# A LoRA layer and a top-2 mixture of experts in one launch: the residual folded into the first layer's weights, x1's two parts taken straight from PSUM, x first on SyncE's queue

## The chip, the cores and the metric

The kernel runs on one core of a Trainium2 chip. The metric is the device time of one launch in microseconds (us). TensorE (PE) multiplies matrices into PSUM, VectorE (DVE) and ScalarE (ACT) work on PSUM and SBUF, GpSimd (POOL) on SBUF only, and SyncE (SP) issues most transfers. Each engine runs its own instructions in order, and the engines meet at semaphores, which the program waits on and raises by hand: nothing reorders the work.

## The reference

Sixteen sequences x of 128 rows by 128 features go through two residual layers, all in float32.

```python
# layer 0, for each sequence b:  W_base, 8 pairs (As[e], Bs[e]) of rank 16, weights cond_8[b, e]
x1 = x + x @ W_base.T + b_base + 2 * sum_e cond_8[b, e] * (x @ As[e].T) @ Bs[e].T
# layer 1: softmax over cond_8[b], the two largest kept and normalised -> w[b, e]
mlp(x1; g, u, d) = (gelu(x1 @ g) * (x1 @ u)) @ d          # 128 -> 512 -> 128
out = x1 + mlp(x1; shared) + sum over the two experts e of b: w[b, e] * mlp(x1[b]; e)
```

## The kernel before

Before anything is computed, layer 0 is rewritten as one weight per sequence: `delta_w(g)` (L906 to L911, on PE) multiplies `a_sb` by `sB`, which is B transposed and scaled by the sequence's weights, for a group g of four sequences (GB = 4, NG = 4 groups), one bank of PSUM each. `w_eff(g)` (DVE) adds the transposed base weight `wT` and leaves the sum in `work`. PE also transposes x itself (`x_transposes`, L904) and ACT copies the result into `xT` (`copy_xT`). Then PE's `first_layer(g)` (L918) multiplies the two into bank 4 + g, and DVE's `first_layer(g)` (L673) adds the bias and the residual `xT` and writes x1 over `xn`. This opening stage ends when x1 is split into a high part (`x1_hi`, float32 rounded to the matmul format) and a low part (`x1_lo`, the remainder). ACT and DVE do that for group 0, ACT and POOL for group 1, and POOL alone for groups 2 and 3, in `x1_split`.

The second stage is the shared MLP. `shared_group(g)` runs over four chunks c of 128 hidden columns, so a step t = 4g + c has three matmuls for the gate and three for the up projection (L985 to L987: high by high, high by low, low by high), and three for the down projection of the chunk two steps earlier (L1001 to L1003). ACT applies gelu, DVE multiplies (`gated`), ACT and DVE split the product (`split_h_hi`, `split_h_lo`). Between these stand parts of a small sort, by POOL and a few tiny matmuls, which deals the 32 pairs of sequence and expert into 12 slots of two sequences that share an expert, and 8 singles. `sort_counts` is the first of them, and DVE packs the lists into words (`pack`), which each engine loads into registers (`read`, L243). In the same stage ACT, DVE and POOL split the experts' weights into `wex`.

The third stage is four singles (`gate_up_single` L1043, `down_single` L1061), then twelve slots (`slot`, L1079 to L1081 and L1101 to L1103), then four more singles and the output. PE's addresses for the first four down projections come from `downs_of(0)`, a read of the word `four_e`. It stands in `shared_group` behind the gate and up matmuls of the last step and ahead of `down_shared(3, 1)`; `downs_of(1)` stands between `gate_up_single(3)` and `down_single(2, ...)`.

SyncE's queue begins with B (`b_nat`, 1,024 runs of 64 bytes), then group 0 of x, W_base, x group 1, the shared gate weights and so on; ACT's queue brings cond_8, As and the bias. ACT loads the table for exp before the router's softmax, and the table for gelu (L541) just before the shared stage.

Of the kernel before, what the change touches and what calls it, by code (L numbers as in the profile page):

```python
# [17 lines left out]
def lora_then_top2_moe(nc, x, cond, W_base, b_base, As, Bs, ex_gate, ex_up, ex_down,  # L18
# [31 lines left out]
    with ExitStack() as ctx:  # L50
# [66 lines left out]
        with nc.sbuf_tensor("sB", [P, 2, GB, H], F32) as sB:  # L117
            pass
# [47 lines left out]
        sB_ready = sem("sB_ready")  # L166
        xT_ps = sem("xT_ps")
# [6 lines left out]
        x1lo_first = sem("x1lo_first")  # L174
        x1lo_later = sem("x1lo_later")
# [78 lines left out]
        def _(sp):  # L254
            sp.dma_start(b_nat[:, :, :], Bs.rearrange("e o r -> o e r")).then_inc(ld_b, 16)
# [75 lines left out]
        def _(pool):  # L331
# [33 lines left out]

            pool.wait_ge(sh_hi, 1)
# [21 lines left out]
            x1_split(1)  # L388
            pool.wait_ge(x1_ready, NG)
# [34 lines left out]
            x1_split(2)  # L424
            up_lo(0, 1)
            x1_split(3)
# [23 lines left out]
            for k in range(2):  # L450
                for i, value in enumerate((top_idxf[:, k:k + 1], bcol[:, 0:1], rt[:, 22 + k:23 + k])):
                    pool.tensor_scalar(rows[:, k, i, :], iota[:, :], lp[:, 12 + k:13 + k], value,
                                       ALU.is_equal, ALU.mult).then_inc(sort_step, 1)
            up_lo(2, 4)
            up_lo(3, 5)
            up_lo(4, 5)
# [24 lines left out]
            pool.wait_ge(x1lo_first, 1)  # L481
            pool.wait_ge(x1lo_later, NG - 1)
# [26 lines left out]
        def _(act):  # L509
            act.dma_start(cond_sb[:, :], cond).then_inc(ld_cond, 16)  # L510
            act.dma_start(a_sb[:, :], As.rearrange("e r c -> (e r) c")).then_inc(ld_a, 16)
# [16 lines left out]
            copy_xT(0)  # L528
            copy_xT(1)
# [3 lines left out]
            copy_xT(2)  # L533
            split_x1_hi(0)

            act.wait_ge(ld_sh_up, 16)
            act.copy(wsh[:, 2 * I:3 * I], raw_sh[:, 1, :]).then_inc(sh_hi, 1)
            copy_xT(3)
            split_x1_hi(1)

            act.activation(rt[:, 24:25], rt[:, 8:9], ACT.Gelu_apprx_tanh).then_inc(gelu_table, 1)  # L541
# [50 lines left out]
            def slot(p, j):  # L592
                for n in range(2):
# [4 lines left out]
                    if n == 0:  # L598
# [11 lines left out]
            act.wait_ge(lists_ready, 2)  # L610
            for p in range(NBUF):
# [9 lines left out]
        def _(dve):  # L621
# [12 lines left out]
            def router_weights():  # L634
# [4 lines left out]
                dve.tensor_scalar(rt[:, 16:18], rt[:, 8:10], rt[:, 2:3], None, ALU.mult).then_inc(rt_step, 1)  # L639
                dve.wait_ge(rt_step, 6)  # L640
# [11 lines left out]
            def scale_B(g, bT=bT):  # L652

                if g >= 2:
                    dve.wait_ge(delta_ps, g - 1)
                dve.tensor_tensor(sB[:, g % 2, :, :],
# [12 lines left out]
            def first_layer(g):  # L669

                dve.wait_ge(x1_ps, g + 1)
                dve.wait_ge(xT_ready, g + 1)
                dve.scalar_tensor_tensor(xn[:, g * GB:(g + 1) * GB, :],  # L673
                                         bank[4 + g][:, :].rearrange("p (b s) -> p b s", b=GB), bias[:, 0:1],
                                         xT[:, g * GB:(g + 1) * GB, :], ALU.add, ALU.add).then_inc(x1_ready, 1)
# [8 lines left out]
            scale_B(1)  # L684
# [505 lines left out]
```

## Time and profile before

| what | value |
|---|---|
| median of 3 runs | 133.23 us (133.16 to 133.29) |
| the profiled execution's own time | 133.25 us |
| its span, first to last instruction | 131.6 us |
| PE busy | 125.8 us, 96% of the span |
| DVE, ACT, POOL busy | 89.9, 70.5, 59.4 us |
| share of PE in the chain that ended last | 86% |
| bytes moved | 26.56 MB, mean 202 GB/s |

The profiled execution's own time is 1.65 us above its span, and 0.02 us above the median, so that a difference worked out in the span can be taken off the median as it is. PE is busy nearly everywhere. What can be won lies in the opening stage, in which PE waits for others and its matmuls are longer, and in the few gaps behind it.

### The profile page before, as it was taken

How to read it: one execution, taken by the hardware profiler on the slowest of the kernel's cores; microseconds unless marked ns; L12 is line 12 of the kernel's file. 1: busy time of each engine (PE TensorE's matmuls, PEld its weight loads, DVE VectorE, ACT ScalarE, POOL GpSimd, SP SyncE). 2: the span in 40 equal slices, each digit the busy share in tenths (PEclk: the TensorE clock that was granted, in tenths of full speed). 3: DMA queues.
4: the chain of work that ended last, by engine and by line, in shares of the span. 5: the costliest groups of instructions: out<-in, count | busy, mean ns of one | idle time of the engine just before them, and what ended most of it. 6: DMA issues, size and time to landing. Idle time of an engine off the chain costs nothing.

```text
span 131.6 us, 3151 instructions
## 1 busy us (share of the span) xinstructions
PE 125.8 (96%) x869; PEld 113.9 (87%) x869; DVE 89.9 (68%) x180; ACT 70.5 (54%) x134; POOL 59.4 (45%) x110
## 2 busy tenths in 40 slices
PE   6999999999999997999989999999999999999991
PEld 6657787878887867999989999999999999999991
DVE  2678879679977888643375677666867686766741
ACT  3431867977856874411284665666566755711110
POOL 5209285497785737352065325633463504610000
PEclk9999999999999999999999999999999999999999
DMA  3997888799100077469835875577599970013921
GB/s 55 278 332 271 229 264 237 237 293 298 47 2 0 0 216 252 143 248 404 344 120 199 319 279 204 202 281 299 199 308 328 396 224 0 2 29 136 272 70 56
DMA packets 14524, 26.56 MB, mean 202 GB/s; under 512 B 2224, under 2 KB 7600, under 8 KB 12976
## 3 DMA queue, kind: packets, MB, share of 16 engines
q1 hardware_dynamic: 14192, 26.35, 60.1%
q8 instruction: 5, 0.08, 0.3%
q10 hardware_dynamic: 320, 0.07, 0.2%
q14 instruction: 7, 0.06, 0.1%
HBM read 12.52 MB, written 1.31 MB: 105 GB/s over the span
## 4 chain that ended last, share of the span: by engine, by line
PE 86%; DVE 4%; issue 4%; DMA 1%; ACT 1%; DVEq 1%; POOL 1%; ACTq 0%; POOLq 0%
PE bank L1043 11%; PE bank L1081 8%; PE bank L1079 8%; PE bank L1080 8%; PE bank L1061 6%; PE bank L985 5%; PE bank L987 5%; PE bank L986 5%; PE bank L1101 5%; PE bank L1103 4%; PE bank L1102 4%; PE bank L1001 3%; PE bank L910 3%; PE bank L1003 3%; PE bank L1002 3%
## 5 line engine op out<-in xcount | busy, mean ns | idle before, releaser
L548 ACT ACTIVATE work<-bank 128x512 f32<-128x512 f32 x48 | 28.7, 598 | 40.2 <-PE bank L1081 18.3
L712 DVE TENSOR_TENSOR bank<-bank,work 128x512 f32<-128x512 f32 x40 | 27.9, 698 | 20.7 <-PE bank L1081 12.2
L477 POOL TENSOR_TENSOR wstd<-wexd,wstd 128x512 fp32r<-128x512 f32 x12 | 15.5, 1295 | 28.2 <-ACT wstd L590 28.2
L729 DVE TENSOR_TENSOR hT_lo<-bank,hT_hi 128x512 fp32r<-128x512 f32 x40 | 27.3, 682 | 1.3 <-issue 0.5
L1079 PE MATMUL bank<-xp,wst 128*128 128x256 f32 x96 | 27.2, 284 | 0.0
L1080 PE MATMUL bank<-xp,wst 128*128 128x256 f32 x96 | 27.2, 283 | 0.0
L1081 PE MATMUL bank<-xp,wst 128*128 128x256 f32 x96 | 27.2, 283 | 0.0
L557 ACT CAST hT_hi<-bank 128x512 fp32r<-128x512 f32 x40 | 23.3, 582 | 2.7 <-PE bank L1003 1.5
L1080 PEld LDWEIGHTS bank<-xp,wst 128*128 128x128 f32 x96 | 18.4, 192 | 0.0
L1079 PEld LDWEIGHTS bank<-xp,wst 128*128 128x128 f32 x96 | 18.4, 192 | 0.0
L1081 PEld LDWEIGHTS bank<-xp,wst 128*128 128x128 f32 x96 | 18.4, 192 | 0.0
L1043 PE MATMUL bank<-xs,sst 128*128 128x128 f32 x128 | 15.6, 275 | 0.0
L1043 PEld LDWEIGHTS bank<-xs,sst 128*128 128x128 f32 x128 | 15.1, 192 | 0.2
L1101 PE MATMUL bank<-hT_hi,wstd 128*128 128x256 f32 x48 | 13.9, 289 | 0.3 <-DVE hT_lo L729 0.3
L1103 PE MATMUL bank<-hT_hi,wstd 128*128 128x256 f32 x48 | 13.6, 283 | 0.0
L1102 PE MATMUL bank<-hT_lo,wstd 128*128 128x256 f32 x48 | 13.6, 283 | 0.0
L385 POOL TENSOR_TENSOR wex<-raw_ex,wex 128x512 fp32r<-128x512 f32 x8 | 10.3, 1288 | 6.7 <-DVE wex L734 6.7
L985 PE MATMUL bank<-x1s,wsh 128*128 128x512 f32 x32 | 12.6, 393 | 0.0
L987 PE MATMUL bank<-x1s,wsh 128*128 128x512 f32 x32 | 12.5, 390 | 0.0
L986 PE MATMUL bank<-x1s,wsh 128*128 128x512 f32 x32 | 12.5, 389 | 0.0
L470 POOL CAST xp<-x1s 128x256 fp32r x24 | 8.9, 398 | 5.1 <-issue 3.9
L720 DVE TENSOR_TENSOR work<-bank,work 128x512 f32<-128x512 f32 x8 | 5.5, 690 | 6.5 <-PE bank L1043 6.5
(154 smaller groups left out, 213.9 us busy)
## 6 DMA issues: line engine op xcount, KB each, us to landing
wst<-wex SPq DMA_DIRECT2D x12, 1024.0 KB, 4.9
raw_ex<-n_L_cond_skill_gate_dram SPq DMA_DIRECT2D x8, 256.0 KB, 3.4
raw_ex<-in_L_cond_skill_up_dram SPq DMA_DIRECT2D x8, 256.0 KB, 4.2
sst<-n_L_cond_skill_gate_dram SPq DMA_DIRECT2D x8, 256.0 KB, 3.2
sst<-in_L_cond_skill_up_dram SPq DMA_DIRECT2D x8, 256.0 KB, 4.1
xn<-in_x_dram SPq DMA_DIRECT2D x4, 256.0 KB, 4.2
out_dram<-xT SPq DMA_DIRECT2D x4, 256.0 KB, 2.7
sst<-_L_cond_shared_gate_dram SPq DMA_DIRECT2D x1, 256.0 KB, 4.0
```

Source lines behind the costliest of these rows:

```text
L548: act.activation(gelu_sb[q], gate_ps[q][:, :], ACT.Gelu_apprx_tanh).then_inc(gelu_done, 1)
L557: act.copy(hT_hi[:, q, :], up_ps[u][:, :]).then_inc(hi_done, 1)
L712: dve.tensor_tensor(up_ps[u][:, :], up_ps[u][:, :], gelu_sb[q], ALU.mult).then_inc(h_done, 1)
L729: dve.tensor_tensor(hT_lo[:, q, :], up_ps[u][:, :], f32(hT_hi[:, q, :]), ALU.subtract).then_inc(lo_done, 1)
L985: pe.matmul(ps[:, :], w_hi, x1_hi(g), start=True, stop=False)
L986: pe.matmul(ps[:, :], w_hi, x1_lo(g), start=False, stop=False)
L987: pe.matmul(ps[:, :], w_lo, x1_hi(g), start=False, stop=True).then_inc(done, 1)
L1043: mm = pe.matmul(ps[:, c * S:(c + 1) * S], sst[:, j, k * I + c * P:k * I + (c + 1) * P], xs[:, s % NBUF, :], start=True, stop=True)
L1079: pe.matmul(of_c, w_hi, x_hi, start=True, stop=False)
L1080: pe.matmul(of_c, w_hi, x_lo, start=False, stop=False)
L1081: mm = pe.matmul(of_c, w_lo, x_hi, start=False, stop=True)
L1101: pe.matmul(ps, w_hi, h_hi, start=(c == 0), stop=False)
```

## The change

- The identity is added to the base weight: `wT` becomes W_base transposed plus I, made by DVE from PSUM and `ident`. The matmul of the first layer then yields x1 less its bias, and the residual isn't added afterwards.
- x1's parts come from the bank itself. ACT's `split_x1_hi(g)` applies Identity with the bias to bank 4 + g for all four groups, and DVE's new `split_x1_lo(g)` computes bank + bias - high. DVE's `first_layer` is gone. x1 as a whole, which is only needed when the shared MLP's sum is added, is put together on POOL, high plus low, in `x1_whole(g)`, in the place of `x1_split`; `sum_group` waits for it.
- `sB` has four buffers instead of two, and POOL scales those for groups 2 and 3 (DVE did). DVE's order changes: five of the seven router operations stand behind `w_eff(0)`, the low part of the shared up weights stands ahead of `split_x1_lo(0)`, and `w_eff(3)` stands right behind the latter.
- `b_nat` moves from the head of SyncE's queue to the second place on ACT's. `sort_counts` moves behind the transposes of x and W_base on PE. ACT's gelu table is loaded between `copy_xT(0)` and `copy_xT(1)`.
- On PE the read `downs_of(0)` moves behind `gate_up_single(0)`. On ACT `down_hi(0, 0)` moves ahead of the first slot.

PE, in the opening: rows of before, in which `b_nat`, `memb_sum`, `xn`, `w_nat` are B, the sort's sums, x and W_base.

```order
L898 MATMUL bank7<-ident,b_nat 128x128 [waits ld_b]
L926 MATMUL bank3<-memb_sum,ltri 16x16 [waits sort_step,consts]
L927 MATMUL bank3<-ones,memb_sum 16x16
L904 MATMUL bank4<-ident,xn 128x128 [waits ld_x0]
L904 MATMUL bank4<-ident,xn 128x128 x3
L952 MATMUL bank6<-ident,w_nat 128x128 [waits ld_w]
L910 MATMUL bank0<-sB,a_sb 128x512 [waits sB_ready,ld_a]
L904 MATMUL bank5<-ident,xn 128x128 [waits ld_x1,setup_sb]
```

The same stretch of PE after the change.

```order
L901 MATMUL bank7<-ident,b_nat 128x128 [waits ld_b]
L907 MATMUL bank4<-ident,xn 128x128 [waits ld_x0]
L907 MATMUL bank4<-ident,xn 128x128 x3
L957 MATMUL bank6<-ident,w_nat 128x128 [waits ld_w]
L932 MATMUL bank3<-memb_sum,ltri 16x16 [waits sort_step,consts]
L933 MATMUL bank3<-ones,memb_sum 16x16
L916 MATMUL bank0<-sB,a_sb 128x512 [waits sB_ready,ld_a]
L907 MATMUL bank5<-ident,xn 128x128 [waits ld_x1,setup_sb]
```

The two matmuls of the sort's sums moved behind the transposes; B's transpose is still the first, ahead of x's.

PE, at the end of the shared stage, before: the last up matmuls, the read of `four_e`, a down projection and the first single.

```order
L987 MATMUL bank2<-x1s,wsh 128x512
L243 TENSOR_LOAD four_e [waits packs]
L243 ISA x2
L1001 MATMUL bank5<-hT_hi,wshd 128x512 [waits lo_done]
L1002 MATMUL bank5<-hT_lo,wshd 128x512
L1003 MATMUL bank5<-hT_hi,wshd 128x512
L1043 MATMUL bank0<-xs,sst 128x128 [waits h_done,st_gu0,lo_done,xs_ready,ld_down]
L1043 MATMUL bank0<-xs,sst 128x128 x3
L1043 MATMUL bank3<-xs,sst 128x128 x4
L1001 MATMUL bank5<-hT_hi,wshd 128x512 [waits lo_done]
```

The same place after the change.

```order
L993 MATMUL bank2<-x1s,wsh 128x512
L1007 MATMUL bank5<-hT_hi,wshd 128x512 [waits lo_done]
L1008 MATMUL bank5<-hT_lo,wshd 128x512
L1009 MATMUL bank5<-hT_hi,wshd 128x512
L1044 MATMUL bank0<-xs,sst 128x128 [waits h_done,st_gu0,lo_done,xs_ready,ld_down]
L1044 MATMUL bank0<-xs,sst 128x128 x3
L1044 MATMUL bank3<-xs,sst 128x128 x4
L243 TENSOR_LOAD four_e [waits packs]
L243 ISA x2
L1007 MATMUL bank5<-hT_hi,wshd 128x512 [waits lo_done]
```

The read, with its wait for DVE's word, now follows the first single's gate and up matmuls.

DVE, before, from the first effective weight to the last.

```order
L664 TENSOR_TENSOR work<-bank0,wT 128x512 [waits delta_ps,setup_sb]
L656 TENSOR_TENSOR sB<-bT,lora_s 128x512 [waits delta_ps]
L664 TENSOR_TENSOR work<-bank1,wT 128x512 [waits delta_ps]
L656 TENSOR_TENSOR sB<-bT,lora_s 128x512 [waits delta_ps]
L673 SCALAR_TENSOR_TENSOR xn<-bank4,bias,xT 128x512 [waits xT_ready,x1_ps,ld_bias]
L664 TENSOR_TENSOR work<-bank2,wT 128x512 [waits delta_ps]
L698 TENSOR_TENSOR x1s<-xn,x1s 128x4x128 [waits x1hi_ready]
L673 SCALAR_TENSOR_TENSOR xn<-bank5,bias,xT 128x512 [waits xT_ready,x1_ps]
L664 TENSOR_TENSOR work<-bank3,wT 128x512 [waits delta_ps]
```

And after.

```order
L673 TENSOR_TENSOR work<-bank0,wT 128x512 [waits delta_ps,setup_sb]
L652 TENSOR_TENSOR rt<-rt 16x1 [waits rt_step]
L654 RECIPROCAL rt<-rt 16x1 [waits rt_step]
L656 TENSOR_SCALAR rt<-rt 16x2 [waits rt_step]
L658 TENSOR_SCALAR rt<-rt 16x2 [waits rt_step]
L660 SCALAR_TENSOR_TENSOR rt<-rt 16x2 [waits rt_step]
L673 TENSOR_TENSOR work<-bank1,wT 128x512 [waits delta_ps]
L673 TENSOR_TENSOR work<-bank2,wT 128x512 [waits delta_ps]
L702 TENSOR_TENSOR wsh<-sst,wsh 128x512 [waits sh_hi]
L680 SCALAR_TENSOR_TENSOR x1s<-bank4,bias,x1s 128x4x128 [waits x1hi_ready,ld_bias]
L673 TENSOR_TENSOR work<-bank3,wT 128x512 [waits delta_ps]
```

Two scalings and two first-layer additions of 512 columns left the stretch, and one weight split came in.

The core of the diff:

```diff
 @block.sync
-            sp.dma_start(b_nat[:, :, :], Bs.rearrange("e o r -> o e r")).then_inc(ld_b, 16)
             sp.dma_start(xn[:, 0:GB, :], x[0:GB].rearrange("b s h -> s b h")).then_inc(ld_x[0], 16)
 @block.gpsimd
+            pool.wait_ge(setup_sb, 2)
+            for g in range(2, NG):
+                pool.tensor_tensor(sB[:, g, :, :],
+                                   bT[:, :].rearrange("p (a o) -> p a o", a=1).to_broadcast([P, GB, H]),
+                                   lora_s[:, g * GB:(g + 1) * GB].rearrange("p (b a) -> p b a", a=1)
+                                   .to_broadcast([P, GB, H]), ALU.mult).then_inc(sB_later, 1)
...
-            def x1_split(g):
-                if g >= 2:
-                    pool.wait_ge(x1_ready, g + 1)
-                    pool.tensor_copy(x1_hi(g), xn[:, g * GB:(g + 1) * GB, :]).then_inc(x1hi_ready, 1)
-                pool.wait_ge(x1hi_ready, g + 1)
-                pool.tensor_tensor(x1_lo(g), xn[:, g * GB:(g + 1) * GB, :], f32(x1_hi(g)),
-                                   ALU.subtract).then_inc(x1lo_later, 1)
+            def x1_whole(g):
+                pool.wait_ge(x1lo_ready, g + 1)
+                pool.tensor_tensor(total[:, g * GB:(g + 1) * GB, :], f32(x1_hi(g)), f32(x1_lo(g)), ALU.add
+                                   ).then_inc(x1_ready, 1)
 @block.scalar
             act.dma_start(cond_sb[:, :], cond).then_inc(ld_cond, 16)
+            act.dma_start(b_nat[:, :, :], Bs.rearrange("e o r -> o e r")).then_inc(ld_b, 16)
...
-                act.wait_ge(x1_ready, g + 1)
-                act.copy(x1_hi(g), xn[:, g * GB:(g + 1) * GB, :]).then_inc(x1hi_ready, 1)
+                act.wait_ge(x1_ps, g + 1)
+                act.activation(x1_hi(g), bank[4 + g][:, :].rearrange("p (b s) -> p b s", b=GB), ACT.Identity,
+                               bias=bias[:, 0:1]).then_inc(x1hi_ready, 1)
...
+            act.wait_ge(exp_done, 1)
+            act.activation(rt[:, 24:25], rt[:, 8:9], ACT.Gelu_apprx_tanh).then_inc(gelu_table, 1)
             copy_xT(1)
...
-                    if n == 0:
+                    if n == 0 and not (isinstance(p, int) and p == 0):
                         down_hi(p, j, down_at(act, 2 * p))
...
             act.wait_ge(lists_ready, 2)
+            down_hi(0, 0, down_at(act, 0))
 @block.vector
-            dve.tensor_copy(wT[:, :], bank[6][:, 0:H]).then_inc(setup_sb, 1)
+            dve.tensor_tensor(wT[:, :], bank[6][:, 0:H], ident[:, :], ALU.add).then_inc(setup_sb, 1)
...
+            def split_x1_lo(g):
+                dve.wait_ge(x1hi_ready, g + 1)
+                dve.scalar_tensor_tensor(x1_lo(g), bank[4 + g][:, :].rearrange("p (b s) -> p b s", b=GB), bias[:, 0:1],
+                                         f32(x1_hi(g)), ALU.add, ALU.subtract).then_inc(x1lo_ready, 1)
...
             def sum_group(g):
                 dve.wait_ge(down_done, NC * g + NC)
+                dve.wait_ge(x1_ready, g + 1)
 @block.tensor
-            sort_counts()
             x_transposes(0)
             pe.wait_ge(ld_w, 16)
             pe.transpose(bank[6][:, 0:H], w_nat[:, :], ident[:, :]).then_inc(setup_ps, 1)
+            sort_counts()
...
                     gate_up_shared(g, c)
-                    if NC * g + c == NU - 1:
-                        pe.wait_ge(packs, P_FOUR_E)
-                        first.extend(downs_of(0))
...
             gate_up_single(0)
+            pe.wait_ge(packs, P_FOUR_E)
+            first = downs_of(0)
             down_shared(NG - 1, NC - 2)
```

## Rows read from the trace of the kernel before

**Rows 1.** The page: engine's busy time, share, instructions; and granted clock by slices.

```profile
PE 125.8 (96%) x869; PEld 113.9 (87%) x869; DVE 89.9 (68%) x180; ACT 70.5 (54%) x134; POOL 59.4 (45%) x110
PEclk9999999999999999999999999999999999999999
```

**Rows 2.** Busy time by stretch (from:to, length, PE, PEld, DVE, ACT, POOL), the slots.

```profile
68.10:117.00 48.90, 48.90 (x408) 48.84 (x409) 34.85 (x68) 29.77 (x56) 21.63 (x32) 1.00 0.62 226
```

**Rows 3.** Chain that ended last, 0 to 12 us: start, us until the next, what.

```profile
0.88 1.71 DMA cond_sb<-in_cond_dram
...
6.14 1.71 PE bank L910 x2
7.85 0.85 PE bank L904 x4
...
10.32 0.89 PE bank L918 x8
11.21 0.86 PE bank L910 x2
```

**Rows 4.** The same chain, 12 to 17 us.

```profile
12.54 0.58 ACT xT L519
13.13 0.53 ACT x1s L524
...
14.95 0.69 DVE work L664
...
15.69 1.16 PE bank L918 x8
```

**Rows 5.** Timeline at the end of the shared stage: PE and DVE.

```profile
48.77 0.39 PE L987 MATMUL bank<-x1s,wsh 128*128 128x512 f32 x1
48.95 0.14 DVE L745 SCALAR_TENSOR_TENSOR four_e<-two_e 1x2 int32<-1x2 int32 x1
...
50.00 0.49 PE L1001 MATMUL bank<-hT_hi,wshd 128*128 128x512 f32 x1 [0.84 <-DVE four_b L745]
50.33 0.39 PE L1002 MATMUL bank<-hT_lo,wshd 128*128 128x512 f32 x1
...
51.66 0.69 DVE L729 TENSOR_TENSOR hT_lo<-bank,hT_hi 128x512 fp32r<-128x512 f32 x1 [0.31 <-ACT hT_hi L557]
```

**Rows 6.** Timeline, PE: the first slot's down projection.

```profile
68.09 0.39 PE L1101 MATMUL bank<-hT_hi,wstd 128*128 128x256 f32 x1 [0.34 <-DVE hT_lo L729]
```

**Rows 7.** Timeline: B's and x's first transfers, start and issue time, on SyncE's queue.

```profile
0.87 0.46 SPq L255 DMA_DIRECT2D b_nat<-in_L_cond_Bs_dram  x1
...
1.39 0.58 SPq L256 DMA_DIRECT2D xn<-in_x_dram  x1
```

**Rows 8.** The same two transfers: size, and us from issue to landing.

```profile
xn<-in_x_dram SPq DMA_DIRECT2D x1, 256.0 KB, 3.2
b_nat<-in_L_cond_Bs_dram SPq DMA_DIRECT2D x1, 64.0 KB, 2.6
```

**Rows 9.** Packets of both queues, 2.8 to 3.0 us: q10 is ACT's, q1 SyncE's.

```profile
q10 hardware_dynamic: 92, 0.04, 73.1%
q1 hardware_dynamic: 78, 0.01, 30.9%
```

**Rows 10.** Timeline, PE alone, the first layer's matmuls of groups 2 and 3.

```profile
14.53 2.31 PE L918 MATMUL bank<-xT,work 128*128 128x128 f32 x16
```

**Rows 11.** Groups by line and form, 4 to 17 us: busy us, mean ns.

```profile
L378 POOL TENSOR_TENSOR x1s<-xn,x1s 128x512 fp32r<-128x512 f32 x1 | 1.5, 1461 | 2.4 <-ACT x1s L524 2.4
```

**Rows 12.** Timeline, PE alone, where the second word is read.

```profile
59.76 1.50 PE L1043 MATMUL bank<-xs,sst 128*128 128x128 f32 x12
61.10 2.35 PE L1061 MATMUL bank<-wexd,work 128*128 x16
```

**Rows 13.** Timeline and landing of the first single's up weights.

```profile
45.95 0.38 SPq L290 DMA_DIRECT2D sst<-in_L_cond_skill_up_dram  x1
...
sst<-in_L_cond_skill_up_dram SPq DMA_DIRECT2D x1, 256.0 KB, 2.8
```

More of the change, by code:

```diff
@@ L115, in lora_then_top2_moe @@
         hT_hi = sb("hT_hi", [P, 2, I], F32R)
-        with nc.sbuf_tensor("sB", [P, 2, GB, H], F32) as sB:
+        with nc.sbuf_tensor("sB", [P, NG, GB, H], F32) as sB:
             pass
@@ L166, in lora_then_top2_moe @@
         sB_ready = sem("sB_ready")
+        sB_later = sem("sB_later")
         xT_ps = sem("xT_ps")
@@ L386, in up_lo @@
                                    f32(wex[:, e * GU + U_HI:e * GU + U_HI + I]), ALU.subtract).then_inc(ex_ulo, 1)
-            x1_split(1)
-            pool.wait_ge(x1_ready, NG)
+            x1_whole(0)
+            pool.wait_ge(x1_ps, NG)
             pool.memset(base[:, :, :], 0.0).then_inc(base_zero, 1)
@@ L423, in _ @@
             pool.tensor_tensor(twice[:, 1:2], twice[:, 2:3], twice[:, 3:4], ALU.add).then_inc(sort_step, 1)
-            x1_split(2)
+            x1_whole(1)
             up_lo(0, 1)
-            x1_split(3)
             up_lo(1, 2)
@@ L453, in _ @@
                                        ALU.is_equal, ALU.mult).then_inc(sort_step, 1)
+            x1_whole(2)
             up_lo(2, 4)
             up_lo(3, 5)
+            x1_whole(3)
             up_lo(4, 5)
@@ L480, in _ @@
             pool.wait_ge(lists_ready, 2)
[L481 to L482 removed]
+            pool.wait_ge(x1lo_ready, NG)
             for s in range(NBUF):
@@ L532, in _ @@
             act.copy(wsh[:, 0:I], raw_sh[:, 0, :]).then_inc(sh_hi, 1)
-            copy_xT(2)
-            split_x1_hi(0)
             act.wait_ge(ld_sh_up, 16)
             act.copy(wsh[:, 2 * I:3 * I], raw_sh[:, 1, :]).then_inc(sh_hi, 1)
+            copy_xT(2)
+            act.wait_ge(ld_bias, 16)
+            split_x1_hi(0)
             copy_xT(3)
             split_x1_hi(1)
-            act.activation(rt[:, 24:25], rt[:, 8:9], ACT.Gelu_apprx_tanh).then_inc(gelu_table, 1)
+            split_x1_hi(2)
+            split_x1_hi(3)
             def gelu(t, q):
@@ L684, in _ @@
             scale_B(1)
+            router_weights()
             dve.wait_ge(setup_ps, 3)
[L686 to L687 removed]
+            dve.wait_ge(consts, 1)
+            dve.tensor_tensor(wT[:, :], bank[6][:, 0:H], ident[:, :], ALU.add).then_inc(setup_sb, 1)
             dve.wait_ge(setup_sb, 3)
             w_eff(0)
[L690 removed]
+            router_sum()
             w_eff(1)
[L692 to L694 removed]
             w_eff(2)
[L697 to L700 removed]
             dve.wait_ge(sh_hi, 2)
@@ L704, in _ @@
                               ALU.subtract).then_inc(sh_lo, 1)
-            first_layer(2)
-            first_layer(3)
+            dve.wait_ge(ld_bias, 16)
+            split_x1_lo(0)
+            w_eff(3)
+            for g in range(1, NG):
+                split_x1_lo(g)
             def gated(t, q, u):
@@ L907, in delta_w @@
             def delta_w(g):
-                pe.wait_ge(sB_ready, g + 1)
-                pe.matmul(bank[g][:, :], a_sb[:, :], sB[:, g % 2, :, :].rearrange("p b o -> p (b o)"),
+                if g < 2:
+                    pe.wait_ge(sB_ready, g + 1)
+                else:
+                    pe.wait_ge(sB_later, g - 1)
+                pe.matmul(bank[g][:, :], a_sb[:, :], sB[:, g, :, :].rearrange("p b o -> p (b o)"),
                           start=True, stop=True).then_inc(delta_ps, 1)
@@ L1004, in down_shared @@
                           ).then_inc(down_done, 1)
-            first = []
             def downs_of(k):
```

35 lines of the change are left out of this document (9 added, 26 removed).

## The prediction

> **What bounds the kernel now.** I read the page first, for the engines' shares: PE is busy 96% of the span, and the next engine, DVE, 68% [rows 1]. The table of stretches then says where that is true: in the twelve slots, 68.1 to 117.0 us, PE is busy for all of the 48.90 us [rows 2]. Nothing that the change does can shorten that stage, nor the singles and the shared stage around it, except by starting them sooner. So I ask of each edit one thing: does PE reach the next stage sooner, or leave out a gap? The chain of waits gives the opening. Up to the first matmul of the shared stage it runs almost wholly through PE, with one detour at 12.5 to 15.6 us through ACT and DVE [rows 3, 4]. Behind the opening, the timeline of PE alone shows two gaps that the change touches, one of 0.84 us at the end of the shared stage [rows 5] and one of 0.34 us at the first slot [rows 6].
>
> One thing about the opening matters for every price. The two passes of a 128x512 matmul of `delta_w` last 1.71 us at 6.14 us and 0.86 us at 11.21 us; those between them start at 8.70 (7.85 + 0.85) and are through at 10.32, so 1.62 [rows 3]. A factor of two is that between TensorE's two levels, 1.2 and 2.4 GHz, although the granted clock is printed at its top digit in all slices [rows 1]. By durations, then, PE works at the lower level until about 10.2 us and at the higher one from there; ahead of the change it had been busy without a gap since 6.14 us. If that moment stays where it is, work that is shifted by d us ahead of it costs or gains only d/2 behind it, since what crosses the moment changes its speed by two.
>
> **The opening, up to the end of delta_w(0).** The order of PE begins with the transpose of B in both kernels, so B's landing now counts. Before, B is issued at 0.87 us and lands 2.6 us later, at 3.47; x's first group is issued at 1.39 and lands 3.2 later, at 4.59 [rows 7, 8]. After, x is issued at 0.87, and B behind cond_8 on ACT's queue, some 0.48 later (the distance by which ACT's second issue follows its first is about that of SyncE's, 0.46 [rows 7]), at 1.35. Lower bound: B lands its old 2.6 us after issue, at 3.95. A middle value: the two transfers are the same bytes, they kept the engines until 4.59 before, and the last of the two is now B, started 0.04 earlier than x was: 4.5. Upper bound: between 2.8 and 3.0 us both queues were served, ACT's with 92 packets and SyncE's with 78 [rows 9]. At 92 in 0.2 us B's 1,024 packets take 2.2 us; with the 1.7 us that the nearly empty cond_8 takes from issue to landing [rows 3] this is 1.35 + 1.7 + 2.2 = 5.2. I take 4.5, since it needs no new rate.
>
> From there PE does B's transpose, four of x (0.85 [rows 3]), that of W_base, and the sort's four small passes. A transpose is a quarter of 0.85, so 0.21 each for B and W_base, and I give the sort's sums 0.2: 4.55 + 0.21 + 0.85 + 0.21 + 0.2 = 6.0. The scaled B is ready in time (transpose, then one DVE operation of about 0.7: 5.8). Delta_w(0) starts at 6.0 to 6.1 and ends at 7.8, against 7.85. By the bounds 3.95 and 5.2 it ends at 7.3 or 8.5. So moving x ahead and the sums behind buys what the later B takes: the term is -0.05 with bounds -0.55 and +0.65 at 7.85 us, and half of them behind 10.2: **-0.02, from -0.28 to +0.33**.
>
> The Trainium skill, "DMA: Bandwidth & Descriptors", section "Queues, rings and completion order", says that each DMA engine takes turns between the rows of queues it has work for, packet by packet. By that rule B shares with x, W_base and x's next group and lands near the upper bound, not at 4.5; the sum would be 0.35 worse. The trace shows both queues served at once in those 0.2 us, but also that ACT's second transfer came while B was already thinning out, so it does not decide.
>
> **The rest of the opening.** Behind delta_w(0) PE has the same work. Before, it finished the third group's first layer and then waited for `w_eff(3)`: DVE ran it at 14.95 to 15.64, and the last four matmuls, eight passes, started at 15.69 [rows 4], while the third group's had started at 14.53 [rows 10] and, at 0.89 for such a set [rows 3], were through at 15.42. DVE was late since two first-layer additions, one x1 split and two scalings lay in its way. After, the wait for `w_eff(3)` begins at delta_w(3)'s end, 14.10 (14.53 less the half of 0.85 for x's transposes at the higher level), or behind `split_x1_lo(0)`: ACT copies the third x group (12.54 to 13.1), takes x1's high part for group 0 (to 13.7), DVE the low part (to 14.45), then `w_eff(3)`, 0.69 long [rows 4], to 15.15. That is before 15.42, so PE's 0.27 us go: **-0.22**, from -0.27 to 0 (cover 0.27 on DVE; the chain through ACT is one extra operation of 0.6 from closing it).
> What the edits put elsewhere costs nothing by these covers: POOL's two scalings, each at most 1.46 as its nearest operation [rows 11], run from about 6 to 9 us, ahead of delta_w(2) at 11.21; the identity takes the place of a copy of the same size; ACT's table load falls into the time between two copies of x, in which ACT had nothing, and leaves the time before the first gelu; ACT's two additional high parts are done by 17.1, and the first product on DVE waits for the gelu anyway; POOL's `x1_whole`, at most 1.46, takes the place of a copy and a subtraction for groups 2 and 3, and each is done microseconds before `sum_group` asks for it. SyncE's other loads come one issue, 0.46, sooner. What would be late next is DVE: its `split_x1_lo(3)` at 17.4 to 18.1 stands right ahead of the first product.
>
> **The read of four_e.** Before, PE's last up matmul starts at 48.77 and the following ones would start at 49.00 and 49.23 (0.23 is the distance of such matmuls). DVE wrote the word at 48.95 to 49.09, and PE's next two started at 50.00 and 50.33 [rows 5]. So the wait and the load of the word cost 50.33 - 49.23 = 1.10. After, the word is long there, and the load stands behind 16 matmul passes of the first single. The nearest case is the second word's read, which stands in just that place behind `gate_up_single(3)`: twelve passes from 59.76 at 0.112 each end at 61.10, and the next line starts at 61.10 [rows 12]. No gap, so the sequencer does the load while PE works off what it has been given. What is late next? `gate_up_single(0)` now wants its up weights at about 49.7: they were issued at 45.95 and took 2.8, so 48.75 [rows 13]. Behind it, the down projection of step 15 needs the low part that DVE started at 51.66 and that also waited for PE [rows 5]; without that wait it follows DVE's packing at about 51.4 and ends at 52.1, and PE asks at 52.17. **-1.05**, from 0 (the load isn't hidden) to -1.10.
>
> **The first slot.** ACT's weight copy leaves the way between the first two gelus. PE's wait of 0.34 [rows 6] ends with DVE's low part, and DVE must first multiply the second half, which waits for PE's up matmuls as well as for the gelu. I take it that these end hardly sooner. **-0.05**, from 0 to -0.3.
>
> **Sum.** -0.02 - 0.22 - 1.05 - 0.05 = -1.34. The profiled execution's span goes from 131.6 to 130.3, its time from 133.25 to 131.9; the median before is 0.02 below it, so **131.9**. With the bounds: best 133.25 - 0.28 - 0.27 - 1.10 - 0.3 = 131.3; worst, B late and half of the DVE cover gone, 133.25 + 0.33 - 0.1 - 0.8 = 132.7.
>
> **Rivals.** (a) B takes turns with SyncE's queue and lands at 5.2: 133.25 + 0.33 - 0.22 - 1.05 - 0.05 = 132.3. For it: both queues are served at once [rows 9]. Against: nothing shown yet. (b) Slower than before: B is late, PE stands idle ahead of it and the rise of the clock comes later too. From 10.2 to 16.6 PE has 6.2 us of work at the higher level; each us by which the rise is later costs 0.5. With a gain of about 1.0 left behind (a), it decides from a rise 2 us later on; at 3 us later the time is 132.3 + 1.5 = 133.8. For it: after the warm-up matmuls PE would stand idle some 0.6 us longer than before, ahead of B. Against: PE's busy stretch before the rise began at 6.14, and begins at 6.0 to 6.8 now. (c) The same the other way: PE's work is denser and the rise comes 2 us sooner; then ACT's and DVE's chain binds after some 0.8: 131.1. (d) The read of four_e is not hidden, as its wait still holds what stands behind it: 133.25 - 0.3 = 132.95.
>
> **How the numbers follow.** The forecast, 131.9, gets 0.56, (a) 0.18, (b) 0.08, (c) 0.08, (d) 0.06; 0.04 is left for what I don't see. The range 131.1 to 132.8 holds the forecast, (a) and (c), and leaves (b), (d) and the rest out. 0.2% is 0.27 us, about what a measurement of this kernel can tell from no change: faster means below 132.96. The forecast, (a), (c) and some of (d) are: 0.85. Same 0.07, slower 0.08.
>
> **What would show it.** B's transpose on PE at 4.5 to 4.6 (at 5.2 or later, rival a); `delta_w` passes of 0.85 each up to about 10.2 and 0.43 after; no gap of PE ahead of the fourth group's first layer; the shared stage's first matmul at 16.3 to 16.4 instead of 16.60; no gap behind the shared stage's last up matmul, and the singles 1.3 us sooner; the gap at the first slot still about 0.3. Wrong would be: a new wait of PE in the opening for `wT` or for x1's low part, a rise of the clock at another time, or a new gap behind `gate_up_single(0)`.

## The result and the profile after

The kernel after takes 132.08 us in the median (131.1 to 132.9), that before 133.04 (132.54 to 133.29) on the same chip: a ratio of 0.9931, 95% interval 0.9907 to 0.9955, or 0.9 us (0.6 to 1.2) less. The profiled execution took 132.08 us with a span of 130.4, against 133.25 and 131.6.

In the page, the engines' shares answer to [rows 1]: PE has the same work in a span shorter by 1.2 us.

```profile
PE 125.2 (96%) x869; PEld 113.7 (87%) x869; DVE 90.4 (69%) x177; ACT 72.3 (55%) x136; POOL 61.4 (47%) x111
PEclk9999999999999999999999999999999999999998
```

All of PE's waits (line, what it waited for, us in total, times, longest) are two in the opening. The two behind it [rows 5, 6] are gone:

```profile
PE bank L895 <- DVE zeros L631: 1.2, 1, 1.2
PE bank L901 <- DMA b_nat<-in_L_cond_Bs_dram: 1.0, 1, 1.0
```

The chain of the opening, after (start, us until the next, what), answers to [rows 3, 4]. L901 is B's transpose, L907 x's, L957 that of `W_base`, L932 and L933 the sort's sums, L916 `delta_w`, L924 the first layer, L991 the shared stage's first product:

```profile
1.35 3.56 DMA b_nat<-in_L_cond_Bs_dram
4.90 0.04 issue
4.95 0.48 PE bank L901
5.42 0.85 PE bank L907 x4
6.28 0.21 PE bank L957
6.49 0.16 PE bank L932 x2
6.65 0.05 PE bank L933 x2
6.70 2.00 PE bank L916 x2
8.71 0.85 PE bank L907 x4
9.56 1.13 PE bank L916 x2
10.69 0.89 PE bank L924 x8
11.58 0.86 PE bank L916 x2
...
15.07 1.91 PE bank L924 x16
16.98 0.23 PE bank L991
```

B landed at 4.91, so `delta_w(0)` begins at 6.70 against 6.14 before, and it took 2.00 us for 1.71. The last 16 passes of the first layer run as one piece of 1.91: the wait for `w_eff(3)` is gone. By the durations (1.13 for a group's two passes, then 0.86) the clock's rise fell at about 10.1 us, where it had been. In the timeline the first product of the shared stage starts at 16.73, against 16.60 before: the opening lost 0.13.

The timeline of PE at the end of the shared stage answers to [rows 5]; the columns are start, us, engine and line, out<-in:

```profile
48.87 0.39 PE L993 MATMUL bank<-x1s,wsh 128*128 128x512 f32 x1
49.10 0.39 PE L1007 MATMUL bank<-hT_hi,wshd 128*128 128x512 f32 x1
...
49.79 1.95 PE L1044 MATMUL bank<-xs,sst 128*128 128x128 f32 x16
51.50 0.48 PE L1007 MATMUL bank<-hT_hi,wshd 128*128 128x512 f32 x1
```

The down products follow the up products by 0.23, and the first single starts at 49.79 in place of 50.79. At the first slot, the row that answers to [rows 6] has no idle time in front of it:

```profile
66.90 0.39 PE L1102 MATMUL bank<-hT_hi,wstd 128*128 128x256 f32 x1
```

Before, that row stood at 68.09. From it to the end of the span it is 63.5 us in both. So the span's 1.19 us are made of four pieces, each the difference of two starts: the opening +0.13; from the first shared product to the first single 33.06 for 34.19, -1.13; from there to the slots' first product 12.62 for 12.41, +0.21; and from there to L1102 4.49 for 4.89, -0.40.

### The profile page after: what moved, and what is told of

Its sections match the earlier page's. It is cut to its first block, busy times and chain, and to the rows that moved or that the text cites. A ratio compares the mean times of both kernels' runs of the same rounds, so it can differ in the third digit from the quotient of the medians.

```text
span 130.4 us, 3154 instructions
## 1 busy us (share of the span) xinstructions
PE 125.2 (96%) x869; PEld 113.7 (87%) x869; DVE 90.4 (69%) x177; ACT 72.3 (55%) x136; POOL 61.4 (47%) x111
## 4 chain that ended last, share of the span: by engine, by line
PE 94%; DMA 3%; issue 0%; ACTq 0%; DVE 0%; DVEq 0%
PE bank L1044 11%; PE bank L1081 9%; PE bank L1080 9%; PE bank L1082 9%; PE bank L1062 6%; PE bank L991 6%; PE bank L993 6%; PE bank L992 6%; PE bank L1102 5%; PE bank L1104 4%; PE bank L1103 4%; PE bank L916 4%; PE bank L1007 3%; PE bank L924 3%; PE bank L1008 3%; PE bank L1009 3%
## 5 line engine op out<-in xcount | busy, mean ns | idle before, releaser
L714 DVE TENSOR_TENSOR bank<-bank,work 128x512 f32<-128x512 f32 x40 | 27.9, 698 | 18.3 <-PE bank L1082 13.0
L731 DVE TENSOR_TENSOR hT_lo<-bank,hT_hi 128x512 fp32r<-128x512 f32 x40 | 27.3, 682 | 1.0 <-issue 0.5
L1102 PE MATMUL bank<-hT_hi,wstd 128*128 128x256 f32 x48 | 13.9, 289 | 0.0
L389 POOL TENSOR_TENSOR wex<-raw_ex,wex 128x512 fp32r<-128x512 f32 x8 | 10.3, 1291 | 7.4 <-DVE wex L736 7.4
L991 PE MATMUL bank<-x1s,wsh 128*128 128x512 f32 x32 | 12.6, 393 | 0.0
L570 ACT CAST wex<-raw_ex 128x512 fp32r<-128x512 f32 x16 | 9.8, 628 | 0.0
```

The source lines that it names most:

```text
L714: dve.tensor_tensor(up_ps[u][:, :], up_ps[u][:, :], gelu_sb[q], ALU.mult).then_inc(h_done, 1)
L731: dve.tensor_tensor(hT_lo[:, q, :], up_ps[u][:, :], f32(hT_hi[:, q, :]), ALU.subtract).then_inc(lo_done, 1)
L991: pe.matmul(ps[:, :], w_hi, x1_hi(g), start=True, stop=False)
L1102: pe.matmul(ps, w_hi, h_hi, start=(c == 0), stop=False)
```

## The experiments

This table has, for each kernel, the ratio of its time to that of the kernel before, measured on the same chip beside it, and from its profiled execution: when the shared stage's first product started, how long it was from there to the first single, and PE's idle time at the first slot's down product. "Held" is GpSimd's `x1_whole(3)` held behind a pack, explained below.

```
kernel                        median  ratio  95% interval    opening  shared  slot
before                        133.0   1                      16.60    34.19   0.34
after                         132.08  0.9931 0.9907-0.9955   16.73    33.06   0
after, again                  132.47  0.9949 0.9927-0.9971   17.38    33.01   0
before, read moved alone      132.15  0.9924 0.9895-0.9952   16.43    33.07   0.48
after, read back              133.39  1.0031 1.0009-1.0053   16.58    34.49   0
after, copy back              133.60  1.0034 1.0011-1.0057   16.63    33.07   0.47
after, copy back, held        132.55  0.9963 0.9935-0.9990   17.51    33.05   0.44
after, B at SyncE's head      131.66  0.9890 0.9856-0.9925   16.42    33.86   0
after, GpSimd behind wT       132.15  0.9942 0.9918-0.9965   16.70    33.03   0
after, 7 products of zeros    132.74  0.9968 0.9941-0.9996   17.06    33.82   0
after, sums ahead of B        132.67  0.9969 0.9948-0.9989   16.89    33.86   0
B at head, sums early         132.22  0.9919 0.9894-0.9943   16.60    33.87   0
B at head, sums early, held   131.04  0.9868 0.9840-0.9896   15.72    33.04   0
the same, w_eff(3) first      131.27  0.9868 0.9840-0.9897   15.97    33.04   0
```

**The kernel after, again.**

> The changed kernel as it is, beside the others of this call. My theory: what the profile showed is stable: B lands about 3.5 us after its issue on ScalarE's queue, PE waits for it about 1 us, VectorE's router operation of 16x2 elements beside GpSimd's scalings takes 0.8 us instead of 0.2, so that PE's second x transposes start about 0.3 us late; shared stage from 16.7 us, span 130.0 to 130.8. Rival: the 0.8 us operation and B's landing are chance of one execution; then B lands at another time, the shared stage starts elsewhere, and the span moves by as much as half of the shift.

It took 132.47 us, ratio 0.9949. Its opening ended 0.65 us later than in the first profile with nothing changed: both passes of the second `delta_w` were still at the lower clock, so the rise came at about 11.3 us:

```profile
9.60 1.71 PE bank L916 x2
```

The same kernel differs by that much between executions, and a profile shows one of them.

**The read of four_e, alone and taken back.**

```diff
 # before, in shared_group, behind gate_up_shared(3, 3):
-pe.wait_ge(packs, P_FOUR_E)
-first.extend(downs_of(0))
 # behind gate_up_single(0):
+pe.wait_ge(packs, P_FOUR_E)
+first = downs_of(0)
```

> The kernel before with one edit: TensorE reads four_e behind the single expert's matmuls, as after does. Theory (the read is worth the gap it filled, and the rest of the change is worth nothing or slightly less): no idle TensorE time at the shared stage's end for four_e (0.84 us there before), 0.9 to 1.0 us under the kernel before, ratio 0.993, which is the whole gain of the change. Rival (the opening's edits carry part of the gain): 0.4 to 0.6 us under the kernel before, ratio 0.996, and the rest of the 0.9 us is then the opening's.

> One part undone: the read of four_e stands again ahead of down_shared(3, 1). My theory: PE waits there 1.1 us again, but in the changed kernel 0.2 of the 1.1 is given back two matmul groups later by the wait for the last low part; so the kernel is 0.9 us slower than the changed one, and most of the change's gain is gone (ratio to the kernel before 0.998 to 1.001). Rival: the read matters 0.3 us or less, as DVE's words come later in any case: within 0.3 us of the changed kernel.

The read moved alone gives 0.9924, 1.0 us, as much as the whole change. The change without it gives 1.0031, 0.4 us (0.1 to 0.7) above the kernel before, but most of that is again the read: in that kernel PE is idle there for 1.18 us instead of 0.84. In both kernels PE's next matmul starts 0.9 us after VectorE has written the word (49.09 to 50.00 before, 49.38 to 50.28 here), and here the word comes 0.34 later against PE's last up matmul, behind two other packs of VectorE that took 0.73 and 0.48 us instead of 0.18 and 0.14; the reason stands in the next part. So the price of the read is shown from both sides, and nothing shows that the rest of the change gains anything: the whole change is not below the read alone (0.9931 and 0.9949 against 0.9924, with intervals that overlap).

In that second profile the clock rose early, at about 9.3 us, and the opening was no better for it, since VectorE's chain bound it. L680 is the low part of x1, L673 `w_eff(3)`, L924 the fourth group's first layer:

```profile
14.27 0.74 DVE x1s L680
15.01 0.61 DVE work L673
15.66 1.16 PE bank L924 x8
```

**B back at SyncE's head.**

```diff
+sp.dma_start(b_nat...)   # ahead of x's first group
-act.dma_start(b_nat...)  # behind cond_8
```

> One part undone: B is again the first transfer of SyncE's queue, x follows. My theory (B's landing sets the start of the whole opening, at half price since the matmuls are at the lower clock until about 10.1 us): B lands at 3.5, PE transposes it at 3.85, x lands at about 4.6, delta_w(0) starts near 5.9 instead of 6.7; the shared stage starts 0.3 to 0.4 us sooner, at 16.35, and the kernel is 0.3 us faster than the changed one. Rival (x ahead pays for B behind): the same time within 0.1 us. Second rival: the clock's rise moves with PE's first dense stretch, then the gain is the full 0.8 us.

131.66 us, ratio 0.9890, which is 0.5 to 0.8 us under the two ratios of the kernel after. Its interval lies below that of the second of them, which was measured on the same chip, and overlaps that of the first. PE waited 0.4 us for x instead of 1.0 for B, and the shared stage started 0.3 us sooner than in the first profile of after. So B's move, which I had priced together with that of the sort's sums at -0.02, costs something: 0.3 us by the openings, and half a microsecond or more by the times, in which the toss described below also counts. But this profile had a wait that the earlier ones had not, and took 132.40 us, the longest of that kernel. In its list of PE's waits:

```profile
PE bank L1007 <- DVE xn L744: 0.5, 1, 0.5
```

VectorE's `sum_group(2)` was late. Its timeline and GpSimd's show why (start, us, engine and line, out<-in); L748 is VectorE's pack of `two_b`, 16 words, L383 GpSimd's `x1_whole(3)`:

```profile
44.31 1.18 DVE L748 SCALAR_TENSOR_TENSOR two_b<-idx 1x16 int32<-1x16 int32 x1
...
44.17 1.30 POOL L383 TENSOR_TENSOR xn<-x1s 128x512 f32<-128x512 f32 x1
```

In the kernel after the two met the other way round, the pack 0.02 us ahead, and it took 0.17:

```profile
44.64 0.17 DVE L748 SCALAR_TENSOR_TENSOR two_b<-idx 1x16 int32<-1x16 int32 x1
...
44.66 1.31 POOL L382 TENSOR_TENSOR xn<-x1s 128x512 f32<-128x512 f32 x1
```

The pack that began second ended with GpSimd's operation (45.49 and 45.47). Where VectorE's later operation is long, it lasts to GpSimd's end and then nearly its own time (0.68 for L736 elsewhere): in the kernel after `wex`'s low part, L736, beside `x1_whole(2)`:

```profile
39.49 1.79 DVE L736 TENSOR_TENSOR wex<-raw_ex,wex 128x512 fp32r<-128x512 f32 x1
...
39.45 1.27 POOL L382 TENSOR_TENSOR xn<-x1s 128x512 f32<-128x512 f32 x1
```

It ends at 41.28, which is 40.72 and 0.56. VectorE's operations that read PSUM (L714, L731, L744) keep their 0.67 to 0.70 beside the same GpSimd work. The Trainium skill, "SBUF — State Buffer", section "SBUF: two separate sides", says that an operation of VectorE with two SBUF inputs and one of GpSimd that reads SBUF take a pair of ports as an exclusive lock for the whole instruction, so that the later one fully blocks. All these rows agree, and I did not weigh that rule when I priced `x1_whole`.

Before the change the same happened, but cost next to nothing. GpSimd's operation ended at 44.77, 0.26 us after the pack had begun, and the pack ended at 44.80:

```profile
42.22 2.55 POOL L385 TENSOR_TENSOR wex<-raw_ex,wex 128x512 fp32r<-128x512 f32 x2 [0.75 <-DVE wex L734]
...
44.51 0.29 DVE L745 SCALAR_TENSOR_TENSOR two_b<-idx 1x16 int32<-1x16 int32 x1
```

So the change put `x1_whole(3)` within 0.2 us of the pack, and which of the two begins first is a toss. With the read of four_e moved, the table shows it in the shared stage's length: 33.0 to 33.1 us where the pack came first, 33.8 to 33.9 where GpSimd did, with nothing between. The toss costs 0.8 us, of which 0.55 is PE's idle time. The other 0.25 are the overlap of PE's matmuls, which last 0.39 and follow each other by 0.23, and a second matmul that comes 0.31 behind the first instead of 0.23. The read of four_e is the same case: 0.84 us of idle time cost 1.10 [rows 5].

By the traces the toss is decided five microseconds earlier, where `x1_whole(2)` meets L736. In the kernel after GpSimd began 0.04 us ahead and VectorE was held, as in the rows above. With B at SyncE's head it was itself held, 1.83 us for 1.27, although the trace has it 0.01 ahead; so near a tie the starts don't tell who came first:

```profile
39.15 1.83 POOL L383 TENSOR_TENSOR xn<-x1s 128x512 f32<-128x512 f32 x1
39.16 0.68 DVE L736 TENSOR_TENSOR wex<-raw_ex,wex 128x512 fp32r<-128x512 f32 x1
```

Counted from the shared stage's start, the pack begins at 27.9 us in every profile. `x1_whole(3)` begins at 27.90 to 27.93 in the five in which VectorE was held at the first meeting, and the pack is just ahead of it; in the four in which GpSimd was held it begins at 27.75 or 27.76, and the pack is late. Between the two stand GpSimd's splits, which wait for VectorE's. So hundredths of a microsecond at the first meeting go with 0.8 us at the end of the stage; no run changed that meeting alone.

**GpSimd's two scalings behind wT.** Ahead of it I had thought that the 2.00 us of `delta_w(0)` and the late second group of x's transposes came from `wT`, which stood behind a small VectorE operation that took 0.82 us in place of 0.22 beside GpSimd's new scalings.

```diff
-pool.wait_ge(setup_sb, 2)
+pool.wait_ge(setup_sb, 3)
 for g in range(2, NG): ... sB[:, g] ...
```

> GpSimd's two scalings of sB wait until VectorE has written wT (one semaphore value more). My theory (the two engines slow each other when both read SBUF): the router operation at L648 takes 0.2 us again instead of 0.8, wT is written 0.6 us sooner, PE's second x transposes follow delta_w(0) without the gap of 0.3 us, the shared stage starts 0.15 us sooner (half of it, for the clock). delta_w(2) at 11.4 us still finds its sB. Rival: L648 is slow for another reason (the wait for exp, a semaphore), then it stays at 0.8 and nothing moves.

The small operation went back to 0.22 us and `wT` came 0.6 us sooner, but `delta_w(0)` kept its 2.00 us and the ratio was 0.9942. That theory fell.

**The sort's sums.** What was left is the weight load. After, the first load of `delta_w(0)` starts with its matmul, behind the short sums. Before, it ran beneath W's transpose.

```diff
+pe.wait_ge(sort_step, S_MEMB)
+(sort_counts' two matmuls)
 pe.wait_ge(ld_b, 16)
 pe.transpose(bank[7]...)      # B
 ...
-sort_counts()                 # behind W's transpose
```

> The kernel after, with the sort's four 16x16 matmuls ahead of B's transpose, in the 1 us in which TensorE waits for B (memb_sum is ready at 4.4 us, B at 4.9). W's transpose then stands right ahead of delta_w(0). Theory (the sums cost their own 0.2 us and leave the first weight load of delta_w(0), 0.3 us, in the open): delta_w(0) takes 1.71 us again and not 2.00, and from the start of W's transpose to the second group of x transposes it is 1.9 us and not 2.4; with the clock's rise at its moment half of the 0.5 us is left, so the time is 0.25 us under the kernel after, 0.5 us if the rise comes sooner with the work. Rival (delta_w(0) is longer because VectorE's second scaling ends later, or because of the two engines' contention for it): delta_w(0) stays at 2.00 us and the time is that of the kernel after less 0.1 us.

In its chain L954 is W's transpose, L920 `delta_w(0)`, L911 x's second group:

```profile
1.35 3.79 DMA b_nat<-in_L_cond_Bs_dram
...
6.51 0.21 PE bank L954
6.72 1.85 PE bank L920 x2
8.57 1.01 PE bank L911 x4
```

From W's transpose to x's second group it is 2.06 us, against 2.43 (6.28 to 8.71) after: most of the 0.5. But B landed 0.2 us later here, the toss at the pack was lost, and the ratio was 0.9969, no gain. The time rejects my number, the rows don't reject the mechanism. With B first and the sums ahead of x, it shows whole:

```diff
+sp.dma_start(b_nat...)        # SyncE's head, as above
 pe.transpose(bank[7]...)      # B
+(sort_counts' two matmuls)
 x_transposes(0)
```

> The kernel after, with B back at the head of SyncE's queue and the sort's sums between B's transpose and x's first group, where TensorE waited 0.4 us for x when B led the queue. Theory: TensorE waits for nothing but x0 ahead of 4.8 us, delta_w(0) starts at 5.9 us and takes 1.71 us, and the time is 0.25 us under the kernel that only has B at the head (131.7 us, ratio 0.989), so 131.4 us, ratio 0.987, the fastest so far. Rival (what the opening gains is lost to VectorE and ScalarE, which bind once TensorE's clock is up): 131.7 us, ratio 0.989, with waits of the first layer for xT or of the shared stage's first products for wsh.

```profile
6.02 0.21 PE bank L954
6.23 1.71 PE bank L920 x2
7.94 0.85 PE bank L911 x4
```

`delta_w(0)` is at 1.71 again and W's transpose to x's second group at 1.92, both as before. Yet the ratio was 0.9919, and the profile had lost the toss (1.18 us for the pack, shared stage 33.87). The eleven times leave a gap between 131.86 and 132.22: five lie at 131.41 to 131.86, six at 132.22 to 132.59, and the profiled execution, at 132.59, is the longest.

**The toss taken away.**

```diff
 up_lo(3, 5)
+pool.wait_ge(packs, P_TWO_B)
 x1_whole(3)
```

> The kernel with B at SyncE's head and the sort's sums early, and GpSimd's x1_whole(3) held until VectorE's pack of two_b is written. Theory (VectorE's small pack, which reads two operands from SBUF, waits out a GpSimd operation of that kind that began before it; it began 0.14 us behind x1_whole(3) in the profiles in which it took 1.18 us, and 0.02 us ahead of it in those in which it took 0.17 us, so the two outcomes change places between executions): the pack takes 0.17 us, TensorE's wait of 0.5 us for sum_group(2) is gone, and the time is 0.3 to 0.5 us under the kernel without the hold, 131.8 us, ratio 0.988, with the executions above 132.2 us gone. Rival (the spread of the executions comes from the clock's rise alone, and the wait is a thing of the profiled execution): ratio 0.992 as without the hold, with the same spread.

```profile
43.63 0.17 DVE L749 SCALAR_TENSOR_TENSOR two_b<-idx 1x16 int32<-1x16 int32 x1
...
43.87 1.29 POOL L383 TENSOR_TENSOR xn<-x1s 128x512 f32<-128x512 f32 x1 [0.34 <-DVE two_b L749]
```

131.04 us (130.93 to 131.56), ratio 0.9868: no execution above 131.6, a spread of 0.6 us where it had been 1.2, and by the ratios 0.7 us less, more than the 0.3 to 0.5 expected. The lock is what the wait was made of, and the toss was in the times, not only in profiles. The median is 0.4 us under even the quickest times without the hold, and how much of that surplus is luck with the clock can't be told: in this profile it had risen by 8.5 us, the earliest seen.

**The first slot's copy.**

```diff
-if n == 0 and not (isinstance(p, int) and p == 0):
+if n == 0:
     down_hi(...)
-down_hi(0, 0, down_at(act, 0))
```

> The kernel after, with the first slot's second copy of down weights back ahead of the split of h in ScalarE's order. Theory (the 0.34 us for which TensorE waited at the slot's second down product was real and on the path): the wait for hT_lo in the first slot is back at 0.34 us, and the time is 0.3 us above the kernel after, ratio to the kernel before 0.996. Rival (the wait was taken over by the next one, as I predicted with 0.05 us): within 0.1 us of the kernel after.

> The kernel after with the first slot's copy back in its old place, as in the run of that edit alone (ratio 1.003, 1.1 us above the kernel after, of which its profile showed 0.5 us as a wait of TensorE for hT_lo), and with GpSimd's x1_whole(3) held until the pack is written. Theory (the other 0.6 us was the pack's wait, which that run's executions mostly had and its profiled one had not): 0.5 to 0.6 us less than without the hold, ratio 0.999, and the wait of 0.5 us for hT_lo stays. Rival (the copy's own cost is 1.1 us and the profiled execution was the odd one): ratio 1.003 again.

The wait for `hT_lo` is back in both profiles, longer than before the change, as it is with the read moved alone (0.48):

```profile
67.33 0.39 PE L1101 MATMUL bank<-hT_hi,wstd 128*128 128x256 f32 x1 [0.47 <-DVE hT_lo L730]
```

With the copy back the ratio rose to 1.0034, 1.1 to 1.4 us above the two ratios of the kernel after, and with GpSimd held as well it was 0.9963, 0.9 us less, where 0.5 to 0.6 was expected, and about the size of the toss. The copy's move is worth 0.4 to 0.5 us by the profiles, and I take the rest for lost tosses; but the profiled execution of the first of them had won (33.07) and was its quickest, so that is argued and not shown.

**Products of zeros.**

```diff
-WARM_UP = 5
+WARM_UP = 7
```

> The kernel after with seven products of zeros in place of five, so that TensorE works until about 4.4 us and is idle for 0.5 us ahead of B instead of 1.0 us. Theory (the moment at which the clock rises hangs on how busy TensorE was before it, and varies for that reason): the rise, at 10.1 and 11.35 us in the two profiles of after, comes at 10.1 us or sooner, and the time is 0.3 to 0.5 us under that of after, ratio 0.990. Rival (the rise does not ask for it, or VectorE and ScalarE bind once it comes sooner, as in the profile in which it came at 9.3 us): ratio 0.993 to 0.995, within 0.2 us of after.

PE's idle time ahead of B fell to 0.5 us, and B landed at 5.2. The rise came at about 10.3 us, no sooner, and the ratio was 0.9968, with the toss lost in the profile. Nothing was gained.

**w_eff(3) first.** In the profile of the held kernel the clock rose so early that PE waited 0.2 us for `w_eff(3)`:

```profile
11.80 0.98 DVE wsh L703
...
13.42 0.74 DVE x1s L681
14.16 0.61 DVE work L674
...
14.81 1.16 PE bank L929 x8
```

The lock has a part in this wait too. The weight split that the change puts ahead of `x1_lo(0)`, L703, ran beside one of GpSimd's (L378, 11.68 to 12.95). It took 1.78 us for the 0.68 of the kernel before, and x1's low part began as it ended, though its high part had been ready since 12.72:

```profile
11.72 1.78 DVE L703 TENSOR_TENSOR wsh<-sst,wsh 128x512 fp32r<-128x512 f32 x1
```

No run takes this one away. The last run changes the order behind it:

```diff
+w_eff(3)
 dve.wait_ge(ld_bias, 16)
 split_x1_lo(0)
-w_eff(3)
```

> The kernel with all three repairs (B at SyncE's head, the sort's sums early, x1_whole(3) behind the pack) and VectorE's w_eff(3) ahead of the first residual part x1_lo(0). In the profile without this swap the clock rose at 8.5 us, TensorE waited 0.2 us for w_eff(3), and x1_lo(0), 0.74 us, stood ahead of it. Theory (with TensorE's clock up early VectorE binds the first layer's end): the wait is gone, the shared stage starts 0.2 us sooner, and the time is 0.2 us under the kernel without the swap, ratio 0.985, where the clock rises early; nothing where it rises late. Rival (x1_lo(0) is late next, for the third product of the shared stage's first group): the same time, ratio 0.987, and a wait for x1s in place of the one for w_eff(3). Both expect the pack of two_b at 0.17 us and no executions above 132 us.

The wait is gone and none for `x1s` took its place, but the clock rose at about 9.4 us here and the ratio is the same, 0.9868. Whether the swap pays where the rise is early was not seen.

## Why the prediction was right, point by point

The forecast was 131.9 and the time is 132.08, within the range. The sum was -1.34, the profiled span gave -1.19 and the medians -0.9. Part of the nearness is luck. The median before was 133.23 when the forecast was made and 133.04 beside the kernel after, so that the same sum would give 131.7 there. And in the span two terms were wrong against each other: the opening came out at +0.13 for -0.24, the first slot at -0.40 for -0.05.

- **The read of four_e, -1.05**: right. The gap is gone, the load is hidden behind 16 passes, the stage is 1.13 shorter, and moved alone the read gives 1.0 us. Rival (d) falls. I also named what is late next, the low part of step 15. PE asked 0.07 us behind it by my working. In fact PE lost 0.2 us there, most of the +0.21 between the first single and the slots, because VectorE did a `gate_lo` and two packs ahead of it and got to it at 51.61:

```profile
51.61 0.69 DVE L731 TENSOR_TENSOR hT_lo<-bank,hT_hi 128x512 fp32r<-128x512 f32 x1
...
52.43 0.43 PE bank L1007
```

- **The opening to the end of delta_w(0), -0.02 with bounds -0.28 and +0.33**: the term failed, at two steps. B's landing was put at 4.5 and came at 4.91 (4.8 to 5.2 in the other profiles with B on ACT's queue), nearer the upper bound, as rival (a) has it. So has the rule of turns in the Trainium skill, "DMA: Bandwidth & Descriptors", section "Queues, rings and completion order". The packets between 3.0 and 3.2 us show both queues served at once, SyncE's (q1) with 106 and ACT's (q10) with 87:

```profile
q1 hardware_dynamic: 106, 0.05, 88.3%
q10 hardware_dynamic: 87, 0.01, 29.2%
```

  And the sort's sums were given 0.2 us; their own time is that (0.16 + 0.05), but they also laid 0.3 us of weight load bare. `delta_w(0)` ended at 8.70 and not at 7.8, 0.85 later than before; half of that behind the rise is +0.43, above my bound.
- **w_eff(3), -0.22**: right in kind, the wait is gone and 0.27 with it. The cover was thinner than in my working, 0.19: `w_eff(3)` ended at 15.77 and PE asked at 15.96. The shared weights' split ahead of it (L702) had taken 1.42 us beside GpSimd's, and in two profiles with an early rise of the clock it took 1.68 and 1.78, and VectorE bound the opening. +0.43 and -0.27 make +0.16, and the timeline shows +0.13.
- **The rule of d/2**: it held in the profile of after, whose rise was where it had been. It is no rule for the median: the rise lay between 8.2 and 11.5 us over the profiles. Rivals (b) and (c) took it for fixed by the kernel, but it moved with the kernel unchanged. The stretch in which PE worked without a gap ahead of the rise also began sooner than I wrote: at 4.62 before, and at 4.95 in the kernel after.
- **The first slot, -0.05**: mis-sized. The wait of 0.34 went whole and the piece became 0.40 shorter. I took it that the second half's product, and not ACT's copy, was what held up the low part; it was the copy, since the wait is back with it in three profiles (0.44 to 0.48).
- **What the edits put elsewhere "costs nothing"**: wrong for `x1_whole`. It was done in time for `sum_group`, the one reader that I looked at, but it may hold the port against VectorE's pack, and then the stage takes 0.8 us more. Two packs behind it are longer as well, 0.72 and 0.48 us, without a wait of PE in the kernel after. The scalings likewise stretched a VectorE operation from 0.22 to 0.82 us, without a price on the path.

Both profiles of the kernel after had won the toss; how often its other executions lost it isn't shown, and so it isn't shown either how much of the 0.4 us between the sum and the medians is this. With B first, the sums early and the toss taken away, the kernel takes 131.0 to 131.3 us, ratio 0.9868, 0.8 to 1.1 us under the kernel after.

## What to carry to other kernels

When work is moved to GpSimd, list VectorE's operations with two SBUF inputs that can run in the same microseconds, the tiny ones too: the later of two takes its place behind the other, and a wait on what VectorE has just written takes the toss out; here it cost nothing. Put tiny matmuls where the engine waits anyhow, not right ahead of a large one, whose weight load they can't cover. Where a median and a profile disagree, compare the lengths of stages over all profiles: a stage whose length takes two levels with nothing between may hold an order of two instructions that is left open, as here. Then look further back for what decides the order.

## What the runs showed of the hardware

- The clock's rise, read from the durations of equal passes, fell at 10.1 and 11.3 us in two executions of the same kernel. PE's idle time ahead of B doesn't order it: 1.0 to 1.1 us went with 9.3, 10.1 and 11.3, and 0.5 us with 10.3. What decides it is open.
- GpSimd is held up too: `x1_whole(2)` took 1.27 us in five profiles, in which it began 0.02 to 0.04 ahead of VectorE's L736, and 1.82 or 1.83 in seven, in which the two began within 0.01 of each other.
- The register load on PE cost nothing behind 16 passes of the first single: the next matmul followed at 51.50 without a gap. Where the read stood ahead of them, PE's next matmul came 0.9 us after the word was written, in both kernels.
- B's 1,024 runs of 64 bytes needed 3.46 to 3.87 us from ACT's queue beside SyncE's loads, and 2.4 to 2.7 at SyncE's head.
